# An eleventh Toeplitz slot in the bias rows' buffer, bias rows summed early and loaded late, and ordered reloads

## What is computed

```python
h = embed(x)                        # rows of four tables, projected, times 16
n = layernorm(h)
x1 = silu(depthwise_conv3(n @ w1.T + w1_b))
s  = ssm(x1)                        # per channel: a causal convolution over the 128 positions
h  = h + (s * silu(n @ v1.T + v1_b)) @ w2.T + w2_b
n  = layernorm(h)
shared = (silu(n @ sw1 + sb1) * (n @ sw3 + sb3)) @ sw2 + sb2
# each token is sent to 2 of 8 experts, chosen by its position alone
routed = sum over its 2 experts e of gelu(n @ w1[e] + b1[e]) @ w2[e] + b2[e]
out = h + (shared + routed / 2) / 2
```

## Time and profile before

| | |
|---|---|
| median of 3 runs | 421.47 us (421.3 to 421.73) |
| profiled execution | 421.4 us, of which the span of the profile is 419.6 us |
| PE busy | 401.8 us, 96% of the span |
| DVE, ACT, POOL busy | 269.6, 242.7, 220.4 us |
| granted TensorE clock | full speed throughout |

### The profile page before, as it was taken

One profiled execution on the slowest core, in us unless ns is written; L12 is line 12 of the kernel. 1 busy time (PEld: TensorE's weight loads), 2 busy tenths in 40 slices (PEclk: granted clock), 3 DMA queues, 4 the chain that ended last, 5 costly groups with the idle time before them and its releaser, 6 DMA issues.

```text
span 419.6 us, 8492 instructions
## 1 busy us (share of the span) xinstructions
PE 401.8 (96%) x2916; PEld 350.8 (84%) x2916; DVE 269.6 (64%) x609; ACT 242.7 (58%) x439; POOL 220.4 (53%) x265
## 2 busy tenths in 40 slices
PE   8899999999989789999999999999999999999996
PEld 3888887878779776888988988988988988888886
DVE  7887989789765698974663663563564554554333
ACT  4779877768885356645535535535536536436442
POOL 6888999820037085996347347346346346434000
PEclk9999999999999999999999999999999999999999
DMA  4462112299969961101301301301301301100101
GB/s 111 123 197 73 41 51 66 79 329 300 320 181 269 296 217 52 51 0 52 102 0 52 100 2 51 100 0 50 100 1 50 100 0 50 50 0 0 52 0 52
DMA packets 32924, 39.01 MB, mean 93 GB/s; under 512 B 3477, under 2 KB 29171, under 8 KB 32768
## 3 DMA queue, kind: packets, MB, share of 16 engines
q1 hardware_dynamic: 29760, 33.12, 25.7%
q0 software_dynamic: 3136, 5.52, 4.6%
HBM read 34.69 MB, written 8.65 MB: 103 GB/s over the span
## 4 chain that ended last, share of the span: by engine, by line
PE 73%; DVE 12%; issue 4%; ACT 4%; POOL 3%; DMA 3%; DVEq 0%; SPq 0%; ACTq 0%; POOLq 0%
PE ps L1259 22%; PE ps L1260 21%; PE ps L1261 21%; PE ps L1357 3%; DMA bias_e<-rows_dram 2%; PE ps L1401 2%; DVE v_sb L1148 1%; DVE sw_lo L1139 1%; PE ps L1308 1%; PE ps L1359 1%; PE ps L1273 1%; DVE x_mid L1123 1%; DVE x_mid L1130 1%; POOL cat L606 1%; DMA cat<-table_dram,x_ids 1%
## 5 line engine op out<-in xcount | busy, mean ns | idle before, releaser
L1196 DVE SCALAR_TENSOR_TENSOR hid_lo<-act_out,hid_hi 128x512 fp32r<-128x512 f32 x64 | 48.7, 762 | 55.9 <-ACT hid_hi L954 55.9
L941 ACT ACTIVATE act_out<-ps,vec 128x512 f32<-128x512 f32 x32 | 22.1, 689 | 89.4 <-PE ps L1261 89.4
L1190 DVE SCALAR_TENSOR_TENSOR act_out<-ps,vec,act_out 128x512 f32<-128x512 f32 x32 | 24.0, 750 | 50.7 <-ACT act_out L941 50.7
L748 POOL TENSOR_TENSOR h_sb<-h_sb,bias_e 128x256 f32<-128x256 f32 x32 | 24.5, 770 | 60.8 <-DVE h2n L1082 60.8
L1259 PE MATMUL ps<-h2nT_hi,sw_hi 128*128 128x512 f32 x128 | 50.0, 391 | 0.0
L1260 PE MATMUL ps<-h2nT_lo,sw_hi 128*128 128x512 f32 x128 | 50.0, 391 | 0.0
L1261 PE MATMUL ps<-h2nT_hi,sw_lo 128*128 128x512 f32 x128 | 50.0, 391 | 0.0
L741 POOL TENSOR_TENSOR zc_lo<-v_sb,zc_hi 128x256 fp32r<-128x256 f32 x32 | 29.8, 931 | 26.5 <-ACT zc_hi L931 26.5
L945 ACT ACTIVATE act_out<-ps,vec 128x512 f32<-128x512 f32 x32 | 22.1, 690 | 34.2 <-PE ps L1261 34.0
L606 POOL DMA_INDIRECT cat<-table_dram,x_ids x32 | 36.3, 1134 | 8.1 <-issue 6.1
L954 ACT ACTIVATE hid_hi<-act_out 128x512 fp32r<-128x512 f32 x64 | 39.7, 622 | 0.0
(11 more groups left out here) (138 smaller groups left out, 1268.3 us busy)
## 6 DMA issues: line engine op xcount, KB each, us to landing
toep_l<-kernel_rows_dram SPq DMA_DIRECT2D x14, 512.0 KB, 6.7
toep_r<-kernel_rows_dram SPq DMA_DIRECT2D x12, 512.0 KB, 7.5
h_rows_dram<-h_ring SPq DMA_DIRECT2D x32, 128.0 KB, 2.1
h_in<-h_rows_dram SPq DMA_DIRECT2D x8, 512.0 KB, 4.4
stage<-w_e_dram POOLq DMA_DIRECT2D x7, 512.0 KB, 3.6
out_dram<-o_sb SPq DMA_DIRECT2D x7, 512.0 KB, 3.2
bias_e<-rows_dram SPq DMA_DIRECT2D x1, 1024.0 KB, 7.8
toep_r<-kernel_rows_dram SPq DMA_DIRECT2D x4, 256.0 KB, 5.9
```

The lines of the kernel that those rows point to most:

```text
L748: nc.gpsimd.tensor_tensor(at, at, bias_e[:, bass.ds(e, 1), :].rearrange("p o c -> p (o c)"), ALU.add).then_inc(h2_biased, 1)
L941: nc.scalar.activation(act_out[:, n % 4, :], ps[bank][:, :], ACT.Silu, bias=vec[:, C_SB1 + j:C_SB1 + j + 1]).then_inc(act_done, 1)
L1190: nc.vector.scalar_tensor_tensor(act_out[:, n % 4, :], ps[bank + 1][:, :], vec[:, C_SB3 + j:C_SB3 + j + 1], act_out[:, n % 4, :], ALU.add, ...
L1196: nc.vector.scalar_tensor_tensor(hid_lo[:, n % 4, :], act_out[:, n % 4, :], 0.5 if kind == SHARED else 0.25, f32(hid_hi[:, n % 4, :]), ALU ...
```

## The change

- **Sum early.** The bias sources come as 8 rows on 8 partitions (four small transfers in group 1, after the first three h stores), DVE sums them in two instructions (steps 5 and 6), ACT scales them in one (step 7), and SP writes the 8 rows to memory. Four ACT scalings of `bias_e`, that of `bias_row`, its 1 MB load and the 17 POOL instructions go.
- **Load late.** The finished `bias_e` (1 MB over all partitions) is loaded behind the last piece of weights, and POOL waits for it before its first `mixer_bias`.
- **Eleventh slot.** `toep_b` has the addresses of `bias_e`. POOL zeroes its upper half at the start of group 3, between `piece_lo(0)` and `power_pair`; SP loads set 10 behind set 9. So sets 11 to 15 are reloads, five in place of six.
- **Ordered reloads.** The first part of set q waits also for the landed second part of set q-2, the second part of q for the first part of q-1. `h_load(0, 0)` waits for set 14 to have landed, the first expert's weights for set 15.
- **w2's bias row** is loaded once, in group 1; `first_row` and its late load go.

```diff
-TRING = TRIGHT + TLEFT
+TRING = TRIGHT + TLEFT + 1
...
+    mem_b = ExitStack()
+    toep_b = sb(mem_b, "toep_b", [P, PAIRS, SEQ, 2, 2], F16, R)
+    mem_b.close()
     bias_e = sb(ctx, "bias_e", [P, RES, D], F32, R)
...
+    b2_at, b2_before = x_sil[0:RES, 3, 0:2, :], x_sil[0:RES, 3, 2:4, :]
+    sb2_rows, bias_rows = x_sil[0:RES, 2, 0:2, :], x_sil[0:RES, 2, 2:4, :]
...
         def toep_load(q):
-            toep_part(q, 0, HALF if q >= TRING else 0)
+            toep_part(q, 0, 0)
             toep_part(q, 1, 0)
+        def reloaded(q, h):
+            sp.wait_ge(reload_in[q - TRING][h], 16)
+        def reload(q):
+            sp.wait_ge(ssm_done, 2 * (q - TRING + 1))
+            if q >= TRING + 2:
+                reloaded(q - 2, 1)
+            toep_part(q, 0, HALF)
+            if q > TRING:
+                reloaded(q - 1, 0)
+            toep_part(q, 1, 0)
...
-        sp.dma_start(bias_row[:, 0:1, :], bass.AP(rows.tensor, D, [[0, P], [D, 1], [1, D]])).then_inc(rows_in, 16)
-        sp.dma_start(bias_e[:, :, :], bass.AP(rows.tensor, 2 * D, [[0, P], [D, RES], [1, D]])).then_inc(rows_in, 16)
+                if i == 1 and r == 0:
+                    bias_part(b2_at, bass.AP(rows.tensor, 2 * D, [[D, RES], *half]))
+                    bias_part(b2_before[1:RES], bass.AP(rows.tensor, 2 * D, [[D, RES - 1], *half]))
+                if i == 1 and r == 1:
+                    bias_part(b2_before[0:1], bass.AP(rows.tensor, (RES + 1) * D, [[D, 1], *half]))
+                    bias_part(sb2_rows, bass.AP(rows.tensor, D, [[0, RES], *half]))
+                if i == 1 and r == 2:
+                    sp.dma_start(w2_bias, bass.AP(rows.tensor, 0, [[0, P], [D, 1], [1, D]])).then_inc(rows_in, 16)
+            if i == 1:
+                sp.wait_ge(bias_scaled, 1)
+                sp.dma_start(h_bias, bias_row[0:RES, 1, :]).then_inc(bias_out, 16)
...
+        sp.wait_ge(top_zero, 1)
+        toep_part(TRING - 1, 0, HALF)
+        toep_part(TRING - 1, 1, 0)
         for q in range(TRING, NQ):
-            sp.wait_ge(ssm_done, 2 * (q - TRING + 1))
-            toep_load(q)
-            if q == NQ - 1:
-                sp.wait_ge(mm_done, 8 * GROUPS)
-                sp.dma_start(first_row[:, :, :], bass.AP(rows.tensor, 0, [[0, P], [D, 1], [1, D]])).then_inc(first_row_in, 16)
+            reload(q)
+        sp.wait_ge(ssm_done, 2 * 7)
+        reloaded(NQ - 2, 1)
+        h_load(0, 0)
...
-        sp.wait_ge(ssm_done, 2 * (TRING - 3))
-        h_load(0, 0)
+        sp.wait_ge(mm_done, 8 * GROUPS)
+        reloaded(NQ - 1, 1)
         for n in range(1, 4):
             piece_in(n)
-        sp.wait_ge(bias_step, BIAS_STEPS)
-        sp.dma_start(w2_bias, bass.AP(rows.tensor, 0, [[0, P], [D, 1], [1, D]])).then_inc(rows_in, 16)
...
         piece_in(8)
+        sp.wait_ge(bias_out, 16)
+        sp.dma_start(bias_e[:, :, :], bass.AP(h_bias.tensor, 0, [[0, P], [D, RES], [1, D]])).then_inc(bias_in, 16)
...
                     piece_lo(0)
+                    nc.gpsimd.memset(toep_b[:, :, 0:HALF, :, :].rearrange("p j t c w -> p j (t c w)").bitcast(F32),
+                                     0.0).then_inc(top_zero, 1)
...
-        pool.wait_ge(bias_scaled, 5)
-        pool.wait_ge(ssm_done, 1)
-        link(nc.gpsimd.tensor_copy(bias_row[:, 1, :], bias_e[:, RES - 1, :]))
-        for e in range(RES - 1, -1, -1):
-            before = bias_e[:, e - 1, :] if e else bias_row[:, 1, :]
-            link(nc.gpsimd.tensor_tensor(bias_e[:, e, :], bias_e[:, e, :], before, ALU.add))
-            link(nc.gpsimd.tensor_tensor(bias_e[:, e, :], bias_e[:, e, :], bias_row[:, 0, :], ALU.add))
...
+                if r == 7:
+                    act.wait_ge(bias_summed, 2)
+                    nc.scalar.mul(bias_row[0:RES, 1, :].rearrange("p (b t) -> p b t", b=2), bias_rows, 0.5).then_inc(bias_scaled, 1)
...
+            if isinstance(i, int) and i == 1 and r == 5:
+                dve.wait_ge(bias_parts_in, 64)
+                nc.vector.tensor_tensor(b2_at, b2_at, b2_before, ALU.add).then_inc(bias_summed, 1)
+            if isinstance(i, int) and i == 1 and r == 6:
+                dve.wait_ge(bias_summed, 1)
+                nc.vector.scalar_tensor_tensor(bias_rows, b2_at, 0.5, sb2_rows, ALU.mult, ALU.add).then_inc(bias_summed, 1)
...
-            pe.wait_ge(toep_in[q % TRING], 32 * (1 + loads))
+            if q < TRING:
+                pe.wait_ge(toep_in[q], 32)
+            else:
+                pe.wait_ge(reload_in[q - TRING][0], 16)
+                pe.wait_ge(reload_in[q - TRING][1], 16)
```

More of the change, by code:

```diff
@@ L101, in sb @@
         return stack.enter_context(nc.sbuf_tensor(name, shape, dt, side=side))
+    h_bias = nc.dram_tensor("bias_rows_dram", (RES, D), F32, kind="Internal").ap()
     R, L = "right", "left"
@@ L201, in _tower @@
     rows_in = sem("rows_in")
-    first_row_in = sem("first_row_in")
+    bias_parts_in = sem("bias_parts_in")
+    bias_out = sem("bias_out")
+    bias_in = sem("bias_in")
+    top_zero = sem("top_zero")
     ident_step = sem("ident_step")
@@ L214, in _tower @@
     bias_scaled = sem("bias_scaled")
-    bias_step = sem("bias_step")
+    bias_summed = sem("bias_summed")
     cat_zero = sem("cat_zero")
@@ L244, in _tower @@
     toep_in = [sem(f"toep_in{s}") for s in range(TRING)]
+    reload_in = [[sem(f"reload_in{q}_{h}") for h in range(2)] for q in range(TRING, NQ)]
     ssm_done = sem("ssm_done")
@@ L418, in toep @@
         slot = q % TRING
+        if slot == TRING - 1:
+            return toep_b[:, :, :, :, :]
         return toep_r[:, slot, :, :, :, :] if slot < TRIGHT else toep_l[:, slot - TRIGHT, :, :, :, :]
@@ L486, in toep_part, with bias_part @@
             dst = toep(q)[h::2, :, t:, :, :].rearrange("p j t c w -> p j (t c w)").bitcast(F32)
-            sp.dma_start(dst, src).then_inc(toep_in[q % TRING], 16)
+            sp.dma_start(dst, src).then_inc(toep_in[q] if q < TRING else reload_in[q - TRING][h], 16)
         def toep_load(q):
-            toep_part(q, 0, HALF if q >= TRING else 0)
+            toep_part(q, 0, 0)
             toep_part(q, 1, 0)
+        def reloaded(q, h):
[8 more added lines that the diff above has]
+            toep_part(q, 1, 0)
+        def bias_part(dst, src):
+            sp.dma_start(dst, src).then_inc(bias_parts_in, 16)
         def piece_in(n):
@@ L503, in _ @@
                 piece_in(0)
-        sp.dma_start(bias_row[:, 0:1, :], bass.AP(rows.tensor, D, [[0, P], [D, 1], [1, D]])).then_inc(rows_in, 16)
-        sp.dma_start(bias_e[:, :, :], bass.AP(rows.tensor, 2 * D, [[0, P], [D, RES], [1, D]])).then_inc(rows_in, 16)
+        half = [SEQ, 2], [1, SEQ]
         for i in range(1, GROUPS - 1):
@@ L762, in mixer_1 @@
             power_step(GROUPS + 1, 1, eps2_done, rstd2_done)
+            pool.wait_ge(bias_in, 16)
             mixer_bias(0, 0, 0)
@@ L788, in mixer, with add_w2_bias @@
                     add_w2_bias(1 - par, times, 2 * g - 3)
-        def add_w2_bias(par, times, g, row=w2_bias):
+        def add_w2_bias(par, times, g):
             if g == 0:
@@ L794, in add_w2_bias @@
             at = h_in[:, par, g, :]
[L795 removed]
+            nc.gpsimd.tensor_tensor(at, at, w2_bias[:, 0, :], ALU.add).then_inc(h_biased, 1)
         def slot(e, par, times, load=True, bias=True):
@@ L806, in slot @@
             expert_split(e + 2, par, times)
-        pool.wait_ge(first_row_in, 16)
+        pool.wait_ge(rows_in, 16)
         for g in range(GROUPS):
-            add_w2_bias(0, 1, g, first_row)
+            add_w2_bias(0, 1, g)
         pool.wait_ge(h_biased, GROUPS)
@@ L850, in cat_hi @@
             if isinstance(i, int) and i == 1 and r >= 4:
-                if r == 4:
-                    act.wait_ge(rows_in, 32)
-                    nc.scalar.mul(bias_row[:, 0, :], bias_row[:, 0, :], 0.5).then_inc(bias_scaled, 1)
-                at = bias_e[:, 2 * r - 8:2 * r - 6, :]
-                nc.scalar.mul(at, at, 0.25).then_inc(bias_scaled, 1)
+                if r == 7:
+                    act.wait_ge(bias_summed, 2)
+                    nc.scalar.mul(bias_row[0:RES, 1, :].rearrange("p (b t) -> p b t", b=2), bias_rows, 0.5).then_inc(bias_scaled, 1)
                 if r == RES - 1:
@@ L1347, in _ @@
         for q in range(NQ):
-            loads = q // TRING
-            pe.wait_ge(toep_in[q % TRING], 32 * (1 + loads))
+            if q < TRING:
[3 more added lines that the diff above has]
+                pe.wait_ge(reload_in[q - TRING][1], 16)
             for j in range(CH):
```

13 lines of the change are left out of this document (removed).

## The result

| | before | after |
|---|---|---|
| median of 7 runs each, us | 421.76 (421.3 to 422.4) | 419.88 (419.12 to 422.14) |
| ratio | | 0.9965 [0.9951, 0.9979] |
| profiled execution, us (span) | 421.4 (419.6) | 422.14 (420.2) |

The kernel became 0.35% faster, about 1.5 us by the ratio. The profiled execution of after is the slowest of its seven; the others took 419.12 to 420.79 us. So its profile shows what the change gave and also a loss at the hand-over that, by the times and clocks of the others, they do not have: its mean granted clock is 0.996, theirs is 0.999 or 1.0.

What follows compares the result with a forecast made beforehand. PE, busy 96% of the span at full clock, was taken as the bound, so only its stalls or late starts could yield time: 421.4 - 2.32 - 0.35 + 0.95 = 419.7 us, range 418.6 to 422.0.

Steps and rivals of the forecast that it cites:

- The gaps: PE's two "issue" gaps in the ssm stage, read as late code, go with the ordered reloads: -2.32 us.
- Rival A: Ssm stage: gaps stay because the DMA engines stay busy; one left 420.8 us, both 422.0 us; chance 0.28.
- The memset: Start of group 3: zeroing toep_b on POOL lies wholly on the path, +0.95 us, bounds 0.5 and 0.96.
- The sign that the prediction named for it: Start of group 3: DVE's wait, 2.22 us before, would be longer by the memset, 0.95 us.
- Bias work in phase A: Groups 1 and 2: POOL gains up to 0.80 us, two DVE sums cost 0.45; net -0.35, bounds -0.80 and +0.94.
- the 0.45 us allowed: Phase A: cost to POOL of two DVE sums, each taken at half of its 0 to 0.47 us.
- The hand-over: Ssm to expert stage: the ordered reloads delay the first expert's weights at no cost, 0 us, bounds 0 to 0.4.
- ACT waits for a DMA at 144 to 147: Hand-over: a wait of ACT or PE for a DMA at 144 to 147 us would show the prediction wrong.
- the second part of set 15 lands before 142: End of the ordered reloads: this landing before 142 us would show the prediction right.
- the landing of (15, second) at 141.0: Last reload part: issued at 135.4 us, landing at 141.0, when the first expert's weights go out.
- rival B: Hand-over: 7.1 us parts land set 15 at 145.2 and make the weights late; 422.2 to 424.2 us; chance 0.10.
- The rest: Remaining work at nothing: bias_e, loaded at about 150 us, lands 17 us before its first use at 177.27.

Runs made afterwards that it cites:

- order_only: The kernel before with the ordered reloads alone, ten slots and six reloads; 421.06 us, ratio 0.998 [0.997, 0.9991].
- no_order: The changed kernel without any wait of SP for a landed reload, eleven slots and five reloads kept; 425.85 us, ratio 1.0025 to before.
- combined_again: Second series of the changed kernel with toep_b's zeroing moved later and the first expert's weights issued right behind h_in; 420.49 us, ratio 0.995.
- combined_sum_late: As `combined`, with the bias sums laid out on 128 partitions and done in sets 4 to 6 of the ssm stage; 419.71 us, ratio 0.9936.
- no_sum: The changed kernel without DVE's two bias-sum instructions, ACT scaling the plain b2 rows; 419.28 us, ratio 0.9943 to before.
- memset_later: The changed kernel with the zeroing of toep_b moved to step 1 of group 3, after that step's gather; 420.63 us, ratio 0.9941 to before.
- again: The changed kernel measured once more without any edit; 422.04 us, ratio 0.9952 to before.
- combined: The changed kernel with toep_b's zeroing moved later and the first expert's weights issued right behind h_in; 419.17 us, ratio 0.9929, in the first series.
- weights_late: The changed kernel with the first expert's weights and two shared pieces held back until the first half of set 15; 423.75 us, ratio 1.0019.
- before_look: The kernel before, no edit, one execution for a second profile of phase A; 422.12 us.

## Why the prediction was right, and where it was not

419.7 us was forecast and 419.88 measured (1.7 us less than before by forecast, 1.5 by the ratio). The ratio's interval is below 1, so the gain is real, but small.

**The gaps (forecast -2.32 us; measured -2.67).** Right in sign, place and cause: both "issue" gaps go with the order (`order_only` has neither, `no_order` brings them back), and they were on the path, since C-B shrinks by as much as they held and a little more. That the gaps are code that had not arrived was a reading of the distance in the prediction; the packet records show it. Rival A, that a busy DMA alone keeps the gaps, falls: at a share of 0.99 PE ran without one. The Trainium skill's rule of turn-taking by packet (DMA: Bandwidth & Descriptors, Queues, rings and completion order) was applied by rival A so that the length of SP's queue would not matter. That application is not borne out: the code's packet starts up to 4.9 us after PE has entered the block before when SP's queue is long, and 2.9 us at most when it is ordered. Through what the long queue delays it is not shown. One thing the prediction did not see: without the eleventh slot the stage gains only 27.50 - 26.07 = 1.43 us. Of the other 1.24 us, 1.08 are PE's wait for the second part of set 15, which the sixth reload makes late.

**The memset (+0.95; measured +0.97).** B-A rose from 41.50 to 42.47 and fell back when the memset was moved. The sign that the prediction named for it was not seen, though: DVE's wait at the start of group 3 is 2.07 us and not some 3.2, because DVE itself came later. POOL's three rows behind each other are what shows it:

```profile
79.45 1.30 POOL L710 TENSOR_TENSOR w_lo<-toep_r,w_hi 128x512 fp32r<-128x512 f32 x1
80.70 0.96 POOL L717 MEMSET toep_b<- 128x1024 f32 x1
81.61 0.72 POOL L648 TENSOR_TENSOR rstd<-rstd,minus_half 128x2 f32<-128x2 f32 x1
```

**Bias work in phase A (-0.35; measured about +0.3).** This is the term of the sum that was mis-sized. POOL's idle time of the earlier trace rows fell from 0.80 to 0.17 us, but the gain was not the whole of it: with ACT's bias work gone, DVE's convolution work came earlier and beside POOL's `kernel_step`s, whose pair ahead of this row took 1.66 us where it had taken 1.31.

```profile
34.42 1.66 POOL L668 TENSOR_TENSOR toep_r<-toep_r,abar 128x256 f32<-128x256 f32 x2
36.25 1.09 POOL L648 TENSOR_TENSOR rstd<-rstd,minus_half 128x2 f32<-128x2 f32 x1 [0.17 <-DVE rstd L1120]
```

From k0 the next gather starts 9.44 us later in before and 9.08 in after, so 0.36 us were won up to there.

Against that, the two sums cost more than the 0.45 us allowed, and probably more than the 0.94 of the bound: 51.00 - 49.58 = 1.4 us by the mean of nine profiles, 51.29 - 50.03 = 1.3 us in the pair of `combined_again` and `combined_sum_late`, 1.0 by the mean of the nine against the latter, and 0.8 by after alone. Net 51.00 - 50.73 = +0.27 us, with ranges of 0.95 and 0.41 us between profiles of one kind: the forecast -0.35 is missed, but whether the net is above nothing is not shown. The Trainium skill's rule (SBUF — State Buffer, Who interferes with whom), by which a DVE instruction with two SBUF inputs and a GpSimd one that reads SBUF exclude each other, pointed the right way: the gain of this part did vanish. Of what POOL paid, 0.42 us is the wait shown at `no_sum`; where the rest went was not found. The half of a bound was a choice where the rule had argued for the whole of it.

**The hand-over (0, bounds 0 and 0.4; measured 2.5 in the profiled execution, -0.1 to +0.2 in three other profiles with the same tail).** The prediction named as signs of being wrong that ACT waits for a DMA at 144 to 147, and as a sign of being right that the second part of set 15 lands before 142. In the profiled execution ACT waited from 146.49 to 149.23, and that part landed at 144.15: both signs spoke against this term. The step that failed there is the landing of (15, second) at 141.0. It was issued at 137.3, since the parts ahead of it took 4.2 to 5.9 us each, and took 6.8 us: landed at 144.15. That is rival B's mechanism at its point of decision (145, less a little), in one execution. A short wait is not rare and costs little: ACT waited 0.71 us in `memset_later` (E-C 53.76) and 1.42 in `no_sum` (53.92), not at all in `again` (53.62), against 53.71 and 53.97 in the two profiles of before. DVE needs its time for the last ten `z_part`s anyway, and POOL, when it starts late, does its four splits without a pause (152.74, 3.28 us). In after these end at 156.02, 9.9 us behind the last copy of y, in before at 156.64, 8.5 us behind it: 1.4 us are lost there, and the rest of the 2.5 comes behind it, where the clock is at half.

**The rest.** `bias_e` went out at 153.19 instead of 150, landed after 6.0 us at 159.2, and was first used at 177.74: harmless, as said.

**The sum from the runs**: -2.67 + 0.97 + 0.27 + 0 = -1.4 us, against -1.5 measured. That the forecast came so close is partly luck: two errors of size, -0.35 at the gaps and +0.6 in phase A, stood against each other.

**A better version.** `combined` measures 0.9929 [0.9915, 0.9944] and 0.995 [0.9921, 0.9978], `combined_sum_late` 0.9936 [0.9908, 0.9964], where the change itself has 0.9965 and 0.9952. The stages say that the moved memset is worth 0.8 us and the moved sums 1.0 to 1.3; the medians show it less sharply: the first `combined` has an interval below that of the first measurement of the change, its second one overlaps with it.

## What to carry to other kernels

An idle time of PE put down to "issue" has to be told apart first. Count the instructions to the next such place, waits included, and look at the packets of the "instruction" queue and at the landings of what the program waits for there: in `no_order` it was late code, in `order_only` late data. Against late code, holding back transfers that are not yet needed helped here. When transfers are chained by landings, put the one that the next stage starts with ahead of the last wait of the chain, for a single slow landing can otherwise hold up that stage. Small work added to an engine that "has room" is to be priced on the engine beside it that sets the pace, and measured by a stage, not by the span.

## What the runs showed that was not expected

- A landing can be long without a full queue: 6.8 us for the last part, while the DMA share in its last 2 us was only about half:

```profile
142.00:144.00 2.00, 2.00 (x56) 2.00 (x54) 1.89 (x5) 0.75 (x2) 0.00 (x0) 1.00 0.52 202
```

- The granted clock fell to 0.50 after PE had stood for 2.40 us (2.09 us in `weights_late`), and PE, at work again from 153.65, had its short steps back from 157.33 on, 3.7 us later. After the idle times of 1.2 us (the gaps of the earlier trace rows) it did not fall. Between these lengths both were seen: in `before_look` it was at 0.50 from 148.1 to 151.5 us, 1.5 us after the gap of 1.95 us had ended, and in `again` behind an idle time of 1.93 us in the start-up; in `no_order` it stayed at 1.00 behind 1.89 us.

```profile
149.00:150.00 1.00, 1.00 (x6) 0.61 (x5) 1.00 (x3) 0.86 (x1) 0.73 (x3) 0.50 0.36 59
```

- Such a stretch at half clock is usual in before: the mean granted clock is 0.996 or less in 57 of its 84 executions in the three series, and in 3 of 17 of the changed kernel (two series, the other executions of which are at 0.998 or above). Where the stretches lie in executions without a profile is not known, nor what they cost: the executions of before with one are 1.4 and 1.6 us slower in the median in two series and 0.1 faster in the third.
- Two executions of one kernel have the same gaps at the same places, with other lengths (1.20 and 1.12 us, 0.54 and 1.95).
- The start-up before POOL's first kernel step took from 28.27 to 32.12 us in profiles of kernels that differ little or nothing until then.
